# A channel-attention kernel on one core: ScalarE's passes in another order, and in the head the second pair's gram ahead of the first pair's scores

## What is computed

```python
xt = x.reshape(b, c, n).transpose(0, 2, 1)            # x is group-normalized here, 32 groups
qkv = xt @ w_qkv
q, k, v = jnp.split(qkv, 3, axis=-1)                  # then split into 8 heads of 24 channels
q = q / jnp.maximum(jnp.sqrt(jnp.sum(q * q, axis=-2, keepdims=True)), EPS)
k = k / jnp.maximum(jnp.sqrt(jnp.sum(k * k, axis=-1, keepdims=True)), EPS)
k = k * temperature
attn = jax.nn.softmax(jnp.einsum('bhpn,bhnq->bhpq', k, q), axis=-1)
out = jnp.einsum('bhnp,bhpq->bhnq', v, attn)
out = out.transpose(0, 2, 1, 3).reshape(b, n, c) @ w_out + b_out
x = x + out.transpose(0, 2, 1).reshape(b, c, H, W)
```

## Time and profile before

| | us |
|---|---|
| median of 3 runs | 363.25 (363.08 to 363.44) |
| the profiled execution | 362.67 |
| its span in the trace | 360.9 |
| TensorE busy | 316.2 (88%) |
| VectorE busy | 283.7 (79%) |
| ScalarE busy | 240.3 (67%) |
| GpSimd busy | 145.6 (40%) |

### The profile page before, as it was taken

The page is one execution under the profiler, slowest core; times in us unless marked ns, Lnnn a source line. Parts: engine busy times, 40 slices in busy tenths (PEclk is TensorE's granted clock), DMA queues, the critical chain, the costliest instruction groups (busy, mean ns, idle before and its releaser), DMA issues.

```text
span 360.9 us, 9414 instructions
## 1 busy us (share of the span) xinstructions
PE 316.2 (88%) x3724; PEld 222.7 (62%) x3724; DVE 283.7 (79%) x703; ACT 240.3 (67%) x432; POOL 145.6 (40%) x129
## 2 busy tenths in 40 slices
PE   0149858999999999999999999999899999999895
PEld 0037645765678656866677656866677567856552
DVE  5899865895989698976989598977989585269874
ACT  1188499747987589748986689748975789640300
POOL 0069669205750178115840378017820576002000
PEclk9999979999999999999999999999999999999999
DMA  7999900005993298716992499627980565014976
GB/s 224 366 310 247 260 25 3 2 36 165 293 331 100 96 285 269 271 53 185 311 314 63 133 289 318 181 89 198 299 318 22 160 195 173 3 46 138 292 225 220
DMA packets 30828, 67.75 MB, mean 188 GB/s; under 512 B 5504, under 2 KB 12096, under 8 KB 30784
## 3 DMA queue, kind: packets, MB, share of 16 engines
q1 hardware_dynamic: 30544, 66.56, 59.6%
q10 hardware_dynamic: 240, 0.59, 0.6%
HBM read 29.38 MB, written 28.31 MB: 160 GB/s over the span
## 4 chain that ended last, share of the span: by engine, by line
issue 27%; PE 24%; ACT 20%; DVE 20%; POOL 5%; DMA 2%; SPq 0%; ACTq 0%; POOLq 0%; DVEq 0%
PE u_ps L1003 12%; ACT h_sb L572 8%; ACT xn L563 7%; DVE x_sb L926 6%; PE g_ps L1003 4%; DVE bnst L787 4%; PE s_ps L1003 4%; ACT tok L610 3%; POOL l_sb L500 3%; DVE pw L919 2%; POOL grs L506 2%; DMA x_sb<-in_x_dram 2%; DVE tq L903 1%; ACT tq L655 1%; DVE g_ps L912 1%
## 5 line engine op out<-in xcount | busy, mean ns | idle before, releaser
L500 POOL TENSOR_TENSOR l_sb<-xn,h_sb 128x768 f16<-128x768 f32 x63 | 102.7, 1645 | 48.5 <-ACT h_sb L572 48.5
L926 DVE SCALAR_TENSOR_TENSOR x_sb<-u_ps,bias,x_sb 128x384 f32<-128x384 f32 x144 | 84.1, 612 | 16.9 <-PE u_ps L1003 16.2
L1003 PE MATMUL g_ps<-tok 128*128 128x64 f16 (+1 forms) x864 | 86.0, 239 | 7.1 <-ACT tok L610 6.9
L610 ACT COPY tok<-u_ps 128x384 f32<-128x384 f32 x144 | 66.7, 481 | 19.9 <-PE u_ps L1057 18.1
L1003 PEld LDWEIGHTS g_ps<-tok 128*128 128x128 f16 x864 | 56.0, 98 | 33.3 <-ACT tok L610 11.9
L563 ACT ACTIVATE xn<-x_sb,rb 128x768 f32<-128x768 f32 x61 | 60.9, 1027 | 21.7 <-POOL rb L512 21.7
L1003 PE MATMUL u_ps<-h_sb,ml 128*128 128x384 f16 (+1 forms) x336 | 72.7, 326 | 0.0
L787 DVE BATCH_NORM_STATS2 bnst<-x_sb 128x6 f32<-128x384 f32 x144 | 69.9, 543 | 3.0 <-DMA x_sb<-in_x_dram 2.9
L572 ACT ACTIVATE h_sb<-x_sb,rb 128x768 f16<-128x768 f32 x63 | 64.1, 1028 | 8.4 <-PE u_ps L1003 6.8
L1054 PE MATMUL u_ps<-id,h_sb 128*128 128x128 f16 x288 | 49.1, 224 | 6.3 <-DVE l_sb L767 5.4
L506 POOL TENSOR_TENSOR grs<-gvar,minus_half 128x3 f32<-128x3 f32 x8 | 7.1, 882 | 107.0 <-DVE gvar L820 107.0
(11 more groups left out here) (149 smaller groups left out, 525.5 us busy)
## 6 DMA issues: line engine op xcount, KB each, us to landing
x_sb<-in_x_dram SPq DMA_DIRECT2D x48, 384.0 KB, 5.5
out_dram<-x_sb SPq DMA_DIRECT2D x48, 384.0 KB, 3.2
out_dram<-x_sb SPq DMA_DIRECT2D x48, 192.0 KB, 3.1
x_sb<-in_x_dram SPq DMA_DIRECT2D x45, 192.0 KB, 4.4
hl<-h_sb SPq DMA_DIRECT2D x48, 96.0 KB, 3.3
hl<-l_sb SPq DMA_DIRECT2D x48, 96.0 KB, 3.1
x_sb<-in_x_dram ACTq DMA_DIRECT2D x3, 192.0 KB, 4.4
w<-in_L_conv_w_qkv_dram SPq DMA_DIRECT2D x1, 288.0 KB, 7.7
```

Of the source, the lines that this page charges most:

```text
L500: nc.gpsimd.tensor_tensor(l_sb[:, par, t, cols], xn[:, c % XN_RING, :], h_sb[:, par, t, cols], ALU.subtract).then_inc(l_ok, 1)
L610: nc.scalar.copy(tok[:, j % TOK_RING, :, :].rearrange("p b n -> p (b n)").bitcast(F32), slot_words(j)).then_inc(tok_a, 1)
L926: V.scalar_tensor_tensor(out=xs, in0=block_ps(n), scalar=bias[:, t:t + 1], in1=xs, op0=ALU.add, op1=ALU.add).then_inc(out_ok, 1)
L1003: return nc.tensor.matmul(dst, lhs, rhs, start=start, stop=stop, skip_group_check=True)
```

## The change

The change alters tables, one place where products are kept, and three waits. No arithmetic is added or removed.

- Steps p = 1 to 6, ScalarE: the passes x4 and h3 change places around "p", and x8 moves from the A half (slot 3) to the end of the B half. In the A half the four passes behind slots 0, 1, 3, 4 become three behind slots 2, 4, 6, and "exp" moves from slot 6 to slot 7. (The B half of p = 0 goes by the same list.)
- GpSimd: "norms" moves behind one more low part (behind l5 in the usual steps, behind l4 in the head).
- VectorE, usual B halves: two "bn" move ahead of "spread". In the head: the second pair's x2 goes from ScalarE to VectorE ("v2", `BY_VECTOR_1` 3), and "wo" ahead of a "bn" and "norms".
- Head, TensorE: "scores" and "squares" of pair 0 leave the B half of p = -1 and stand behind slots 1 and 2 of the A half of p = 0; "flip" goes from slot 3 to slot 6. So the second gram may start before them: two of pair 0's weighted products are kept in bank 1 of `s_ps` and in the last bank of `u_ps`, not in `g_ps`, `gram` of pair 1 waits for `pw_ok` in place of `pl_ok`, and transposes(1, 3) and "scores" wait for `pl_ok`.
- A half of p = 0, ScalarE: nine passes (h4 to h8, x5 to x8) stand among the slots, where seven did, and they come later; "exp" goes from slot 6 to slot 7.

```diff
-ACT_A = {0: ["h6"], 1: ["h7"], 3: ["x8"], 4: ["h8"], 6: ["exp"], 11: ["v"], 14: ["m"]}
-ACT_B = ["x0", "x1", "x2", "h0", "h1", "t2", "t0", "t1", "h2", "x3", "h3", "p", "x4", "h4", "x5", "h5", "x6", "x7"]
+ACT_A = {2: ["h6"], 4: ["h7"], 6: ["h8"], 7: ["exp"], 11: ["v"], 14: ["m"]}
+ACT_B = ["x0", "x1", "x2", "h0", "h1", "t2", "t0", "t1", "h2", "x3", "x4", "p", "h3", "h4", "x5", "h5", "x6", "x7", "x8"]
...
-FIRST_PE_B = {0: ["gram"], 2: ["w0"], 7: ["w1", "scores", "squares"]}
+FIRST_PE_B = {0: ["gram"], 2: ["w0"], 7: ["w1"]}
...
-FIRST_ACT_B = ["h0", "h1", "x2", "h2", "t2", "t0", "t1", "x3", "p", "h3", "x4", "h4", "x5"]
-FIRST_POOL_B = ["power", 0, 1, 2, 3, "norms", 4, 5, 6, 7, 8]
+FIRST_ACT_B = ["h0", "h1", "h2", "t2", "t0", "t1", "x3", "h3", "x4", "p"]
+FIRST_POOL_B = ["power", 0, 1, 2, 3, 4, "norms", 5, 6, 7, 8]
...
-BY_VECTOR_1 = 2
+BY_VECTOR_1 = 3
...
-SECOND_PE_A = {3: ["flip"], 10: ["v"], 13: ["m"]}
-SECOND_ACT_A = {0: ["h5"], 1: ["x6"], 2: ["h6"], 3: ["x7"], 4: ["h7"], 5: ["x8"], 6: ["exp"], 7: ["h8"], 12: ["v"], 15: ["m"]}
+SECOND_PE_A = {1: ["scores"], 2: ["squares"], 6: ["flip"], 10: ["v"], 13: ["m"]}
+SECOND_ACT_A = {2: ["h4"], 3: ["x5", "h5"], 5: ["x6"], 6: ["h6"], 7: ["x7", "exp"], 8: ["h7"], 9: ["x8", "h8"], 11: ["v"], 14: ["m"]}
...
+            if q == 0 and k < 2:
+                return (s_ps[:, 1, 0:2 * C], u_ps[:, RING - 1, 0:2 * C])[k]
             return xn[:, k, 0:2 * C] if q == PAIRS - 1 else t_ps(k)
...
+                if q == 1 and j == RING - 1:
+
+                    pe.wait_ge(pl_ok, 3)
...
-                    need(pe, pl_ok, 3 * q)
+                    need(pe, pw_ok if q == 1 else pl_ok, 3 * q)
...
                     pe.wait_ge(wm_ok, 2)
+                    pe.wait_ge(pl_ok, 3)
```

More of the change, by code:

```diff
@@ L70 @@
 PE_B = {0: ["gram"], 1: ["sums"], "in 4": ["w0"], "in 7": ["w1"], 11: ["scores"], 13: ["squares"]}
-ACT_A = {0: ["h6"], 1: ["h7"], 3: ["x8"], 4: ["h8"], 6: ["exp"], 11: ["v"], 14: ["m"]}
-ACT_B = ["x0", "x1", "x2", "h0", "h1", "t2", "t0", "t1", "h2", "x3", "h3", "p", "x4", "h4", "x5", "h5", "x6", "x7"]
-POOL_B = ["power", 0, 1, 2, 3, 4, "norms", 5, 6, 7, 8]
+ACT_A = {2: ["h6"], 4: ["h7"], 6: ["h8"], 7: ["exp"], 11: ["v"], 14: ["m"]}
+ACT_B = ["x0", "x1", "x2", "h0", "h1", "t2", "t0", "t1", "h2", "x3", "x4", "p", "h3", "h4", "x5", "h5", "x6", "x7", "x8"]
+POOL_B = ["power", 0, 1, 2, 3, 4, 5, "norms", 6, 7, 8]
 VEC_A = {0: ["soft_in"], 3: ["soft_out"], 7: ["v"], 11: ["m0"], 13: ["m1"], 17: ["stats"]}
-VEC_B = {0: ["gram"], 1: ["var"], 3: ["z"], 5: ["t2"], 7: ["t0", "t1"], 10: ["lo"], 13: ["norms"], 17: ["spread", "bn", "bn", "bn", "bn"]}
+VEC_B = {0: ["gram"], 1: ["var"], 3: ["z"], 5: ["t2"], 7: ["t0", "t1"], 10: ["lo"], 13: ["norms"], 17: ["bn", "bn", "spread", "bn", "bn"]}
 FIRST_PE_A = {17: ["sums"]}
-FIRST_PE_B = {0: ["gram"], 2: ["w0"], 7: ["w1", "scores", "squares"]}
+FIRST_PE_B = {0: ["gram"], 2: ["w0"], 7: ["w1"]}
 FIRST_ACT_A = {1: [6, 7], 2: [9], 3: [10], 4: [12], 5: [13], 6: [14]}
-FIRST_ACT_B = ["h0", "h1", "x2", "h2", "t2", "t0", "t1", "x3", "p", "h3", "x4", "h4", "x5"]
-FIRST_POOL_B = ["power", 0, 1, 2, 3, "norms", 4, 5, 6, 7, 8]
+FIRST_ACT_B = ["h0", "h1", "h2", "t2", "t0", "t1", "x3", "h3", "x4", "p"]
+FIRST_POOL_B = ["power", 0, 1, 2, 3, 4, "norms", 5, 6, 7, 8]
 FIRST_VEC_A = {17: ["bn"] * 7 + ["stats"]}
-FIRST_VEC_B = {0: ["var", "gram", "wm", "v0", "v1", "z", "t2", "t0"],
-               1: ["t1", "lo", "bn", "norms", "wo", "spread", "bn", "bn", "bn"]}
+FIRST_VEC_B = {0: ["var", "gram", "wm", "v0", "v1", "z", "v2", "t2", "t0"],
+               1: ["t1", "lo", "wo", "bn", "norms", "spread", "bn", "bn", "bn"]}
 FIRST_BN = (0, 2, 2, 2, 1)
@@ L990, in step @@
                             mixed_weights()
-                        elif what in ("v0", "v1"):
+                        elif what in ("v0", "v1", "v2"):
                             second_value(int(what[1]))
```

## The result

The changed kernel takes **374.18 us** (median of four executions, 373.05 to 374.85), where the kernel before, run beside it, takes 363.22. The ratio is 1.0298, with an interval from 1.0283 to 1.0314: 11 us slower. The prediction was 375.5 us in a range of 370.4 to 378.0. The profiled execution took 373.05 us with a span of 371.2; before it was 362.67 and 360.9.

What follows compares the result with a forecast made beforehand. Usual periods were taken as bound by TensorE (busy 38.54 of 39.88 us), the head by waits between engines and TensorE's low clock. Head +11.3 and usual steps +1.0 on 363.25 gave 375.5 us, range 370.4 to 378.

Steps and rivals of the forecast that it cites:

- Step 1: Head: transposes(1, 0) start at 51.0, the low clock lasts until 55.9, and "squares" end at 58.5.
- Step 2: Head: transposes(1, 6) wait for l5, held behind "norms" on GpSimd; TensorE goes on at 62.4 after 3.5 us of nothing.
- Step 3: Head: chain through "flip", "exp" and ScalarE's passes to l8; transposes(1, 12) at 73.5 in place of 67.3, +6.2 us.
- step 4: Head: TensorE's clock falls low again after idle stretches, +2.3 us ahead of "flip" and +2.0 us at the end.
- The second term: Head: the clock low again at the end, after little work between slot 7 and transposes 12, +2.0 us.
- step 5: Tail of the head's A half: ScalarE does "v" and "m" ahead of the copies of slots 12 and 15, +0.8 us.
- The usual steps: p = 1 to 6: copy waits go, but late "flip" and "exp" delay "v"; +0.24 us a period, +1.0 us in sum.
- The rule to weigh: Head: by the VectorE-GpSimd port rule v2 and l1 wait for each other; l2 ends 0.65 us later, 375.8 us.
- The clock stays up: Rival: TensorE's idle stretches don't lower its clock, 371.3 us; chance 0.22, together with the clock low only once.
- The usual steps win: Rival: "exp" is no later and the two copy waits come back, 370.4 us; chance 0.10.
- the bound that I had named: Usual steps: if the softmax chain were hidden, the two waits come back whole, 6 x 0.68 = -4.1 us.

Runs made afterwards that it cites:

- Experiment 3: Changed kernel with GpSimd doing low part l5 ahead of the norms in the head: 369.54 us, ratio 1.017.
- experiment 5: Experiment 3's kernel with the passes h7, x8 and h8 ahead of "exp" on ScalarE in the A half of p = 0: 366.86 us, ratio 1.0105.
- Experiment 4: Changed kernel with 56 unread matmuls on TensorE ahead of each of the waits for l5 and l8: 371.02 us, ratio 1.0211.
- Experiments 4 and 6: The latter is experiment 5's kernel with 48 unread matmuls on TensorE ahead of the wait for l8: 364.45 us, ratio 1.0037.
- experiments 9: Kernel before with ScalarE's and GpSimd's new usual-step tables, VectorE's usual B-half table as before ("spread" ahead of all four "bn"): 361.19 us, ratio 0.9948.
- experiments 9 and 10: The latter is the former's kernel with "exp" ahead of pass h8 on ScalarE in the usual A half: 359.13 us, ratio 0.9889.
- experiment 1: Kernel before with only the four usual-step tables changed (ScalarE A and B, GpSimd B, VectorE B): 363.7 us, ratio 1.0011.
- experiment 7: Changed kernel with the second pair's x2 back on ScalarE (no v2 on VectorE): 374.6 us, ratio 1.0317.

## Why the prediction was right, step by step

The time, the sign and the mechanism came out as forecast, and no step of the sum failed by more than about 1 us. By the medians the sum was 1.3 us too high. By the stages of the traces it was 2.4 too high (+12.3 against +9.9). The 1.1 us between the two are luck: 0.5 us lie ahead of the second power, where the forecast has nothing, and 0.6 come from the profiled execution of the kernel after, which lies further below its median (1.1) than that of the kernel before (0.6). Times here are on the axis of before (0.49 us taken off in the head, 10.41 in the usual step).

- **Step 1, TensorE earlier.** Transposes(1, 0) at 51.44 (forecast 51.0), "squares" done at 58.07 (58.5). The low clock ended 3.1 us after the work resumed, not 4.7. So a start that was 0.4 late and a clock that came back early made up for each other.
- **Step 2, transposes(1, 6) wait for l5.** They wait 3.49 us (3.5) and start at 62.03 (62.4). Experiment 3 takes the cause away, and with it 4.1 us of the long stretch.
- **Step 3, the chain to l8.** From "flip" to "exp" 2.85 us (2.9), from "exp" to the end of l8 5.47 (5.5). Experiment 3 leaves "exp" in its place, and its second stall stays (3.03 us); experiment 5 moves the passes ahead of "exp", and transposes(1, 12) come 2.7 us sooner behind transposes(1, 6). Without the 1.3 us of the clock (step 4), transposes(1, 12) came 5.8 us later than before, against 6.2.
- **Step 4, the clock.** This is the term that was mis-sized. I put the low stretch ahead of "flip" at 4.7 us of work, +2.3; it lasted until about 65, and "flip" came 3.98 us behind transposes(1, 6) in place of 2.7: +1.3. Experiment 4 shows that it is the clock: 2.67 us with the same wait and the clock kept. The second term and **step 5** (the tail) were right: from transposes(1, 12) to the next power it took 15.95 us where it was 13.3, +2.7 against 2.8. Experiments 4 and 6, with the clock at 1.00 there, take 14.05 and 14.04: so 1.9 us are the clock (2.0) and 0.8 the tail (0.8). Transposes(1, 12) were thus at 74.47, and not at the 75.8 (73.5 + 2.3) of the forecast.
- **The usual steps.** The two waits of 0.34 us are gone, "flip" starts at 140.00 (140.04), and "v" waits 0.79 us (about 1). But "exp" is at 144.67, not 144.87, and "v" at 147.53, not 147.74: +0.08 us a period, not +0.24. I let "flip" take 0.51 us of TensorE before gram 1. It takes 0.37 (150.41 to 150.78); in the kernel before, gram 1 started 0.51 behind it since it waited for ScalarE's copy, and the two waits that I meant to remove were not the only ones. In experiments 9 and 10, too, gram 1 starts 0.34 us behind "flip". The same holds for experiment 1, whose waits (0.23 and 0.79) are those of the kernel after.
- **The rule to weigh.** The Trainium skill ("SBUF - State Buffer", section "Who interferes with whom") says that VectorE in a two-port mode and GpSimd exclude each other from a shared port pair, and that the one that comes second blocks fully. By that rule v2, which began at 46.95 while l0 ran, waits for l0, and l1 waits for v2, and the trace agrees: v2 took 1.74 us in place of 0.67 and l1 1.95 in place of 1.65. In which mode v2 ran, no run shows. The rule named the place rightly; the 0.65 that I gave it was 0.3.
- **The rivals.** "The clock stays up" is refuted, since the idle stretches did lower it. It named a real term, of 1.3 and 1.9 us where I had 4.3. That experiment 4 is at 371.0, where this rival had 371.3, is chance: its trace still has two low stretches, and its second fill costs 1.2 us. "The usual steps win" needed "flip" to be on time: experiments 9 and 10 have it so and gain 2.0 and 4.1 us, and the last is the bound that I had named, -4.1. That it is the same number is chance: "exp" stands a pass earlier there than in the change, and a wait of 0.46 us is left before "v".

## What to carry to other kernels

In an engine that works in order, an instruction whose input is late costs not its own wait but the readiness of all behind it: before moving work on one engine, look on each other engine for what stands right behind the instruction that this work releases. In a stretch where engines wait for each other, each long idle time of TensorE is to be priced twice, with the low clock that follows it (idle times of 3.0 to 3.5 us cost 1.3 to 1.9 us more here). If such a wait is filled with matmuls of no use, they have to end before it does. And measure the parts of a many-sided edit apart: here ScalarE's new order was worth 2 us in the usual steps, and 4 with "exp" a pass earlier, and could not be seen in the sum.

## What the runs showed of the hardware

- Where an instruction of VectorE and one of GpSimd slowed each other, VectorE lost more, both times: v2 was 1.07 us longer and the low part beside it 0.30. In the kernel before, the two passes `wol<-wo,woh` (L730) took 1.55 us beside the power, which took 1.99 us in place of 1.67; in the kernel after, where nothing of GpSimd runs beside them, they take 0.88.
- The time at the low clock behind a wait isn't fixed. After idle times of 3.48, 3.49 and 3.03 us in the kernel after, TensorE's clock was back at 1.00 some 3.1, 2.8 and 4 us after it resumed; in experiment 7, behind an idle time of 3.16 us, it stayed at 0.50 through the stretches from 51 to 57 us, 5.5 us of work. Nor is the point at which it falls: 2.9 us into the second of these idle times, but only some 0.6 us after the work had resumed in experiment 4 (behind 2.25 us of idle time at "exp"). What decides that, these runs don't show.
- Matmuls of no use kept the clock at 1.00 in both waits that they filled from the high level on (56 took 3.29 us, 48 took 2.84), which was worth 1.3 us at "flip" and 1.65 behind transposes(1, 12). Begun at the low level, 56 took 4.21 us and ran 1.2 us past the wait; the clock was back at 1.00 before they ended, and 1.9 us were gained behind them.
